# Gathers of a max pass: the wait ahead of each is for the gather two places back instead of four

## What is computed

```
def _sage_pool_layer(x, src, dst, Wp, bp, Ws, Wn, b, n_nodes):
    m = jax.nn.relu(x @ Wp + bp)
    msgs = m[src]
    agg = jax.ops.segment_max(msgs, dst, num_segments=n_nodes)
    agg = jnp.where(jnp.isfinite(agg), agg, 0.0)
    return x @ Ws + agg @ Wn + b
```

## Time and profile before

| | |
|---|---|
| median of 3 runs | 2891.17 us |
| lowest and highest | 2879.86 and 2897.45 us |
| profiled execution | 2871.62 us |
| its span, first to last instruction | 2869.9 us |
| mean granted TensorE clock in it | 0.89 |
| busy in the span: TensorE, VectorE, ScalarE, GpSimd | 2447.4, 1805.2, 1187.8, 1128.0 us |
| gathers of the two passes | 640, 664.5 us on GpSimd |

### The profile page before, as it was taken

One profiled execution on the slowest core, in us unless ns is written; L12 is line 12 of the kernel. 1 busy time (PEld: TensorE's weight loads), 2 busy tenths in 40 slices (PEclk: granted clock), 3 DMA queues, 4 the chain that ended last, 5 costly groups with the idle time before them and its releaser, 6 DMA issues. The chain is left out here.

```text
span 2869.9 us, 70218 instructions
## 1 busy us (share of the span) xinstructions
PE 2447.4 (85%) x27871; PEld 1951.2 (68%) x27871; DVE 1805.2 (63%) x5324; ACT 1187.8 (41%) x2826; POOL 1128.0 (39%) x1407
## 2 busy tenths in 40 slices
PE   6778999985888888666888888368799999999999
PEld 4445777763555665434656655258699999999998
DVE  6997999986677777535877777241244444444444
ACT  5997888874434444422444444231221111111110
POOL 4005999983666666436666666310000000000000
PEclk7557999996898999877999999569999999999999
DMA  5103000003454555523555545539400000000000
GB/s 161 41 2 98 13 12 13 12 27 110 123 135 125 128 140 136 135 75 85 143 132 135 142 124 144 164 108 328 141 2 2 2 2 2 2 2 2 2 2 18
DMA packets 156204, 227.27 MB, mean 79 GB/s; under 512 B 59488, under 2 KB 121659, under 8 KB 155202
## 3 DMA queue, kind: packets, MB, share of 16 engines
q1 hardware_dynamic: 129390, 184.69, 21.5%
q0 software_dynamic: 22944, 36.72, 6.5%
q10 hardware_dynamic: 3540, 1.30, 0.2%
HBM read 122.26 MB, written 100.35 MB: 78 GB/s over the span
## 5 line engine op out<-in xcount | busy, mean ns | idle before, releaser
L1886 POOL DMA_INDIRECT max_row<-table,max_src_rows x640 | 664.5, 1038 | 445.0 <-issue 163.2
L2490 PE MATMUL prop<-g,adj 128*128 128x192 f16 x9216 | 770.6, 246 | 7.1 <-PEq L2161 7.1
L2490 PEld LDWEIGHTS prop<-g,adj 128*128 128x128 f16 x9216 | 759.5, 98 | 14.9 <-issue 12.4
L1913 PE MATMUL max_far<-adj 128*96 128x512 f16 x1800 | 543.7, 404 | 14.0 <-issue 12.0
L1758 POOL TENSOR_SCALAR e<-e 128x512 f32<-128x512 f32 (+1 forms) x625 | 365.8, 604 | 198.6 <-ACT e L1746 180.9
L2035 DVE TENSOR_SCALAR adj<-adj,node_numbers 128x512 f16<-128x512 f16 x900 | 306.2, 352 | 200.0 <-PE max_far L1913 120.7
L1772 DVE TENSOR_TENSOR e<-e,a_ps 128x1024 f32<-128x1024 f32 (+1 forms) x313 | 372.2, 1194 | 32.9 <-PE a_ps L1684 13.2
L2579 ACT ACTIVATE g<-prop_state 128x96 f16<-128x96 f32 (+1 forms) x375 | 106.0, 283 | 635.0 <-DVE prop_state L2547 635.0
L1746 ACT ACTIVATE e<-s_ps 128x512 f32<-128x512 f32 (+1 forms) x625 | 335.5, 585 | 60.3 <-PE o_ps L1696 38.5
L2545 DVE SCALAR_TENSOR_TENSOR part<-prop,coef,prop_base 128x96 f32<-128x96 f32 x384 | 120.5, 314 | 313.0 <-PE prop L2490 226.2
L1913 PEld LDWEIGHTS max_far<-adj 128*96 128x96 f16 x1800 | 214.4, 136 | 93.9 <-issue 29.1
(11 more groups left out here) (280 smaller groups left out, 3352.6 us busy)
## 6 DMA issues: line engine op xcount, KB each, us to landing
weights<-max_rows_w SPq DMA_DIRECT2D x52, 400.0 KB
rows_dram<-max_out SPq DMA_DIRECT2D x100, 192.0 KB
weights<-adj SPq DMA_DIRECT2D x48, 400.0 KB
ws_w<-weights SPq DMA_DIRECT2D x50, 384.0 KB
max_same<-same_dram SPq DMA_DIRECT2D x196, 96.0 KB
rows_dram<-adj SPq DMA_DIRECT2D x96, 192.0 KB
ws_w<-weights SPq DMA_DIRECT2D x50, 288.0 KB
max_row<-table,max_src_rows POOLq DMA_INDIRECT x640
```

Of the source, the lines that this page charges most:

```text
L1886: nc.gpsimd.indirect_dma_start(row[i % RING][:, j, :], None, table_dram, bass.IndirectOffsetOnAxis(ap=src_rows[:, 4 * n + j:4 * n + j + 1] ...
L1913: mm = nc.tensor.matmul(far_ps[j % 2][0:D, :], parts[:, k, a, :], hot[(T * j + k) % HOTS], start=k == a == 0, stop=k == T - 1 and a == 1)
L2490: return nc.tensor.matmul(sums(step, t), adj[:, k, t * P:(t + 1) * P], states[:, k, :], start=start and t % 2 == 0, stop=k == END - 1 and ...
```

## The change

Each gather now waits for the landing of the gather two places back. In a block's first two places (j = 0, 1) that is place j + 2 of the block before; in its last two (j = 2, 3) it is place j - 2 of the same block. So two gathers are under way at most, where there could be four. The number of gathers, their order, buffers and semaphores stay, as do all other waits; the first block, whose gathers waited for nothing, now waits twice.

```
--- before.py
+++ after.py
@@ -1880,9 +1880,11 @@
 
                     pool.wait_ge(turned, i - RING + 1)
                 for j in range(4):
-                    if i >= 1:
-
-                        pool.wait_ge(gathered[j], 16 * i)
+                    if j >= 2:
+
+                        pool.wait_ge(gathered[j - 2], 16 * (i + 1))
+                    elif i >= 1:
+                        pool.wait_ge(gathered[j + 2], 16 * i)
                     nc.gpsimd.indirect_dma_start(row[i % RING][:, j, :], None, table_dram,
                                                  bass.IndirectOffsetOnAxis(ap=src_rows[:, 4 * n + j:4 * n + j + 1], axis=0)
                                                  ).then_inc(gathered[j], 16)
```

## The result

The changed kernel takes 3049.40 us (median of 4 runs, 3043.96 to 3061.82) beside 2885.52 us for the kernel before: a ratio of 1.057, 95% interval 1.0536 to 1.0603. The profiled execution took 3048.91 us with a span of 3047.2 us, 177.3 us more than the profiled one of before.

What follows compares the result with a forecast made beforehand. TensorE was taken to set the passes' pace before, gathers afterwards. Pass 1 grows by 32 us and pass 2 by 71 us, less 8 us for shorter lives: +95 us on 2891.2 us, 2986 us, range 2905 to 3065 us.

Steps and rivals of the forecast that it cites:

- The bound and its change: In both passes TensorE sets the pace before; afterwards GpSimd's gathers, two in flight at most, set it.
- Rival B: Passes: fewer gathers in flight shorten each other's life, slack takes all the wait; +0, 2891 us, stragglers to +45; chance 0.27.
- Rival C: Passes: TensorE waits in most steps, half the slot waits stay, its clock may fall; +185 us, 3076 us; chance 0.10.
- A: The forecast itself: life stays near 3.2 to 3.4 us, GpSimd's pace sets each pass; 2930 to 3050 us; chance 0.60.
- The size: Added time of both passes together: 103 us less 8 us, so +95 us.
- the pace of two in flight: Passes: time per gather with two at most, (life + restart) / 2: 1.735 us in pass 1, 1.83 us in pass 2.
- life: A gather's time from issue to landing, sampled at twenty instants a pass by packets: 3.19 us in pass 1, 3.38 in pass 2.
- restart: On GpSimd, from a release to the start of the waiting gather: 0.28 us, read behind TensorE's max_col matmuls.
- The correction of 8 us for shorter lives: Passes: gathers issued later miss part of a large store, so their life shortens; 8 us taken off.
- 555 us of pass 1: Forecast length of pass 1: 320 gathers at 1.735 us, 32 us more than before.
- 586 us of pass 2: Forecast length of pass 2: 320 gathers at 1.83 us, 71 us more than before.
- The rule: Skill page's figure for one such gather, about 2.1 us by estimate, at which the change would cost nothing.

Runs made afterwards that it cites:

- e_one: Kernel before, but each gather waits for the one just before it, so one in flight at most; 3932.52 us.
- e_first_pass: Changed wait in the first pass alone, the wait of before in the second; 2857.47 us beside 2700.86 us for the kernel before, ratio 1.058.
- e_ring5: Changed kernel with five ring buffers for gathered blocks instead of four; 3013.47 us beside 2698.03 us for the kernel before, ratio 1.1146.
- e_slow_issue: Kernel before, four in flight, with a GpSimd memset ahead of every gather of the passes; 2897.43 us beside 2698.03 us.
- e_sixteen: Kernel before with a semaphore per ring place and no landing wait, up to 16 in flight; ratios 1.0006 and, in a second run, 1.0044.
- e_pairs: Two in flight at most, but a pair's first gather waits for both of the pair before, its second for nothing; 3489.56 us.

## Why the prediction was right, and by how much it was off

**The bound and its change: right.** TensorE set the pace before; gathers set it now. Gathers still cost 1.01 us each on GpSimd; the slot waits vanish; all the cost is in the passes; two gathers in flight at most at 222 instants. Rival B (not slower) was right that fewer in flight live shorter, and fails on the pace (below). Rival C was right that TensorE's clock falls with the waiting (0.89 to 0.85) and wrong in what it costs: its 32 us of extra busy time per pass lie inside some 280 us of waiting, and 5 us of slot waits are left, not half. The measured 3049 us are nearer to C's price of 3076 us than to the forecast's 2986 us all the same, and at the upper edge of A's own 2930 to 3050 us: the mechanism was A's, the size was not.

**The size: +175 us against +95.** The term at fault is the pace of two in flight, (life + restart) / 2, of which the restart was put too low. It says that a place stands empty between two gathers only for the restart of 0.28 us. Landings show more. A landing is read as in `e_one` above, as the last recorded update of a gather's semaphore. The changed kernel's own profile has only two thirds of these updates (3362 and 3359 of 5120), that of the kernel before about a quarter, so I take them from passes that have nearly all (5090 of 5120 and more) and nearly the same pace. Empty is the time from a landing to the start of the gather that waited for it:

| mean us | `e_one`, pass 1 | `e_first_pass`, pass 1 | `e_ring5`, pass 1 | `e_ring5`, pass 2 |
|---|---|---|---|---|
| in flight at most | 1 | 2 | 2 | 2 |
| pace of the gathers | 3.25 | 1.90 | 1.89 | 1.92 |
| issue to landing | 2.87 | 3.21 | 3.20 | 3.22 |
| empty | 0.38 | 0.58 | 0.58 | 0.62 |
| gathers whose landing came before the gather ahead was written | 0 of 319 | 122 of 318 | 122 of 318 | 120 of 318 |
| their places empty | none | 0.90 | 0.90 | 0.97 |

*Restart, forecast 0.28 us.* For three of the four gathers of a block it is right: 0.26 us behind the landing. The first of each block takes 0.74 us when it has to wait. The mean of 0.38 us makes (0.38 - 0.28) x 160 = 16 us a pass.

*Order, not in the forecast.* GpSimd issues in order. A gather whose own landing is there must still wait until the one ahead of it has had its landing and is written, and its place stands empty meanwhile. With one in flight this cannot happen; with two it happens to 122 gathers of 318 and adds 0.58 - 0.38 = 0.20 us to each place's mean (0.24 in pass 2 of `e_ring5`), 32 to 38 us a pass. This is the largest thing missing.

*Life, forecast 3.19 and 3.38 us.* The 3.20 to 3.22 us of the table are close to it, which is luck: two errors cancel. If the 32nd packet is taken for all 320 gathers in each pass of the kernel before, and not at twenty instants, the visible life is 2.86 and 2.98 us, so the sample was 0.33 and 0.40 us too high. But the last packet starts before the landing, by 0.37 us on average in `e_one`, 0.45 us in pass 1 of `e_first_pass` and 0.51 us in `e_slow_issue` with its four in flight, so the life that the wait sees was too low by about as much. The changed kernel's visible lives are 2.76 and 2.77 us, 0.10 and 0.21 us shorter than before. In the one profile of `e_first_pass` a life to landing is 3.70 us with four in flight and 3.21 us with two, and in `e_one` it is 2.87 us with one. The correction of 8 us for shorter lives had the right sign and was too small.

The forecast's 555 us of pass 1 become 555 + 16 + 32 and 3 us for the life, 606 us (`e_first_pass` 610.0, the changed kernel 601.1). Its 586 us of pass 2 become 586 + 16 + 38 - 26 = 614 us (`e_ring5` 617.6, the changed kernel 611.9). For rival B the same empty time moves the life below which two in flight are free from 2.99 us to 2 x 1.636 - 0.58 = 2.69 us in pass 1; not even a gather alone in flight has so short a mean life.

Counted by packets as in the earlier trace rows, at 110 and 112 instants of the changed kernel's passes, 168 and 173 gathers were in flight, 1.53 and 1.54 on average, and never more than two. The first and last count of pass 1 and the last of pass 2 (packets on GpSimd's queue; gathers issued):

```profile
q0 software_dynamic: 256, 0.39, 12.6%
...
max_row<-table,max_src_rows POOLq DMA_INDIRECT x9
...
q0 software_dynamic: 10080, 15.50, 13.4%
...
max_row<-table,max_src_rows POOLq DMA_INDIRECT x317
...
q0 software_dynamic: 10112, 15.55, 13.2%
...
max_row<-table,max_src_rows POOLq DMA_INDIRECT x317
```

**The rule.** The quiet gather fits the Trainium skill's figure ("DMA: Bandwidth & Descriptors", section "Anatomy of one DMA — SWDGE (gpsimd) path", 2.1 us by an estimate from it) by its packets, 2.1 to 2.3 us. To its landing by the semaphore the quickest took 2.4 us, the median one 2.5 us and the mean one 2.9 us (`e_one`), and the quiet cycle is 2.71 us. For a limit on what is in flight the mean cycle counts, 3.25 us here.

**What stays open.** Why the kernel before takes 2700 us in some sessions and 2870 to 2900 us in others. A session runs on one chip; whether it is the chip that differs or something else about the session was not separated. The record numbers the chip 2 in the first session (2874 us) and in the second (2698 us), 1 in the third and 15 in the fourth; it does not say whether number 2 is the same chip both times. The profiles differ as well: that of the kernel before in the slower kind of session has 11,900 semaphore updates by DMAs, that of `e_first_pass` 25,800. Whether this goes with the lost time or only with the recording is open. Where it is slow, and the earlier trace rows have waits that end by "remote", semaphores of TensorE that come later than the last matmul's recorded end, and TensorE's clock in the passes is 0.89 to 0.90. In the quick pass with four in flight there is no such wait, and the clock is 0.95. GpSimd in it:

```profile
POOL max_row L1887 <- issue: 80.2, 263, 0.3
POOL max_row L1887 <- DMA max_row<-table,max_src_rows: 42.4, 51, 3.4
...
POOL max_row L1887 <- PE max_col L1903: 1.5, 5, 0.3
```

There TensorE is so quick that even four in flight leave 42 us of landing waits and next to no slot waits. Whether `e_sixteen` would gain there was not tried: it ran twice in the other kind of session. No version that beats both kernels was found.

## What to carry to other kernels

Before limiting what is in flight, compare two paces: that of the consumer (here 1.61 to 1.64 us a gather) and (issue to landing + landing to next issue) / places. Read both from the semaphore, since counting packets misses what lies between the last packet and the landing, 0.37 us on average with one in flight and 0.45 us with two. A run with one in flight gives a lower bound and no more: its 3.25 us, halved, are 1.63 us and would have made two in flight free, where 1.88 us were measured, because the life grows with what else is in flight (2.87 to 3.21 us) and because places that are served in order wait for each other (0.2 us each time). An average in flight of 1.8 under a limit of four does not mean that a limit of two is free: two places held 1.7 gathers (3.21 / 1.896), and not two. And a wait that eats slack is free up to the slack and then costs in full: three in flight cost 1%, two 5.7%, one 37%.

## What the hardware showed that I had not expected

Waiting makes TensorE's work itself longer: the 3293 matmuls of a pass keep it busy for 398 us at a granted clock of 0.96, 430 us at 0.89, 462 us at 0.85, 528 us at 0.78 (`e_pairs`) and 577 us at 0.72 (`e_one`). It cost little or nothing here: the engine waited for gathers for 277 and 303 us of the changed kernel's passes, and the gathers' pace accounts for their length.

A second wait ahead of a gather is not free when the gather has to wait, even if the other semaphore was reached long before: it started 0.26 us behind the landing with one wait, 0.74 us with two (the first of each block in `e_one`) and 0.74 to 0.77 us in `e_pairs`.

The same kernel's time differed by 6.5 to 7% between sessions (2698 and 2701 us; 2874 to 2889 us), while passes set by GpSimd's landing waits differed by 1 to 2%. A ratio measured in one session need not hold in another when the change moves the bound from one engine to another: 1.057 here, about 1.115 there.
